# A recommender tower on one Trainium2 core: block writes on ScalarE's queue, first rows in runs of 24, 8 and 7 fields, gathers placed between lows, dense block loaded in turn 30

## The reference, cut to what matters

```python
e = jnp.stack([tbl_0[ids[:, 0]], ..., tbl_38[ids[:, 38]]], axis=1)          # (2048, 39, 16)
for idx, (W, b) in enumerate([(w0, b0), (w1, b1), (w2, b2)]):               # x0 = xk = e at first
    z = relu(jnp.einsum('bhd,bkd,hks->bsd', x0, xk, W) + b[None, :, None])   # s = 128
    if idx != 2: xk = z[:, :64, :]; direct.append(z[:, 64:, :])
    else: direct.append(z)
h = jnp.concatenate([jnp.sum(jnp.concatenate(direct, 1), axis=-1), dense_ctx], axis=1)   # 256 + 16
y = relu(relu(h @ W_top1 + b_top1) @ W_top2 + b_top2) @ W_top3
```

## Time and profile before

| what | us |
|---|---|
| median of 3 runs (2551.67 to 2557.73) | 2557.03 |
| the profiled execution: its own time | 2558.01 |
| the profiled execution: span from first to last instruction | 2556.2 |
| PE busy, of the span | 2407.8 (94%) |
| DVE busy | 2251.4 (88%) |
| POOL busy | 1689.2 (66%) |
| ACT busy | 1058.5 (41%) |
| first squared product on DVE starts at | 99.11 |
| layer 2 of turn 0, 1, 2, 3, 4, 5 read out by ACT at | 209.7, 292.4, 365.3, 442.0, 515.0, 587.4 |
| the same of turn 30 and 31 | 2413.6, 2496.4 |

### The profile page before, as it was taken

The page is one execution under the profiler, slowest core; times in us unless marked ns, Lnnn a source line. Parts: engine busy times, 40 slices in busy tenths (PEclk is TensorE's granted clock), DMA queues, the critical chain, the costliest instruction groups (busy, mean ns, idle before and its releaser), DMA issues.

```text
span 2556.2 us, 30130 instructions
## 1 busy us (share of the span) xinstructions
PE 2407.8 (94%) x7702; PEld 1448.5 (57%) x7702; DVE 2251.4 (88%) x1657; ACT 1058.5 (41%) x1053; POOL 1689.2 (66%) x1059
## 2 busy tenths in 40 slices
PE   0389999999999999999999999999999999999889
PEld 0145665555666565655666555556665565666556
DVE  0279998999999999999999999999999998999973
ACT  0133444444444444444444444444444443444345
POOL 7267676776767677776768777677768776444330
PEclk9999999999999999999999999999999999999989
DMA  7547998788899888888898888888988887898810
GB/s 185 123 97 183 215 200 192 184 192 198 194 214 202 196 198 194 200 192 199 199 215 194 196 201 191 201 193 199 216 200 201 190 199 162 198 211 198 185 42 11
DMA packets 177592, 470.31 MB, mean 184 GB/s; under 512 B 33972, under 2 KB 68148, under 8 KB 177230
## 3 DMA queue, kind: packets, MB, share of 16 engines
q1 hardware_dynamic: 155249, 462.10, 78.3%
q0 software_dynamic: 19968, 5.15, 2.0%
q10 hardware_dynamic: 2286, 2.23, 0.4%
HBM read 457.02 MB, written 12.33 MB: 184 GB/s over the span
## 4 chain that ended last, share of the span: by engine, by line
PE 67%; POOL 12%; issue 8%; DVE 3%; DMA 1%; ACT 0%; POOLq 0%; SPq 0%; ACTq 0%; DVEq 0%
PE zacc_a L1011 28%; PE zacc_b L1011 26%; POOL low L643 6%; POOL landed L621 5%; PE zacc_a L1046 5%; PE zacc_b L1046 5%; DMA x_thrice<-in_w_top1d 1%; DVE prod L911 1%; DVE low L866 1%; POOL mark L627 1%; PE zacc_b L1043 0%; PE zacc_a L1043 0%; DVE zacc_a L915 0%; DVE prod L915 0%; PE maps L1053 0%
## 5 line engine op out<-in xcount | busy, mean ns | idle before, releaser
L643 POOL TENSOR_TENSOR low<-prod,high 128x1024 fp32r<-128x1024 f32 x384 | 944.8, 2470 | 610.6 <-ACT high L798 604.1
L911 DVE TENSOR_TENSOR prod<-spread,maps 128x2048 f32<-128x2048 f32 x448 | 1016.8, 2281 | 94.1 <-issue 25.5
L798 ACT ACTIVATE high<-prod 128x1024 fp32r<-128x1024 f32 (+1 forms) x576 | 596.1, 1056 | 717.7 <-DVE prod L911 385.2
L1011 PE MATMUL zacc_a<-prod,w_plain 128*128 128x512 f32 (+2 forms) x1536 | 708.8, 596 | 47.1 <-DVE prod L896 41.2
L621 POOL DMA_INDIRECT landed<-in_tbl,rows_id x585 | 631.3, 1079 | 166.4 <-issue 150.8
L1011 PE MATMUL zacc_b<-prod,w_plain 128*128 128x512 f32 (+2 forms) x1536 | 709.0, 596 | 5.9 <-DVE prod L911 5.9
L1011 PEld LDWEIGHTS zacc_a<-prod,w_plain 128*128 128x128 f32 (+2 forms) x1536 | 291.9, 190 | 318.1 <-issue 290.7
L1011 PEld LDWEIGHTS zacc_b<-prod,w_plain 128*128 128x128 f32 (+2 forms) x1536 | 292.1, 190 | 276.4 <-issue 248.9
L896 DVE TENSOR_TENSOR prod<-shifted,x_thrice 117x1024 f32<-117x1024 f32 (+1 forms) x224 | 265.4, 1221 | 88.6 <-DMA shifted<-x_periods 72.9
L1046 PE MATMUL zacc_b<-low,w_high 128*128 128x512 f32 x672 | 283.0, 502 | 14.8 <-POOL low L643 8.6
L1046 PE MATMUL zacc_a<-low,w_high 128*128 128x512 f32 x672 | 280.6, 498 | 6.8 <-POOL low L643 6.8
(11 more groups left out here) (103 smaller groups left out, 1627.8 us busy)
## 6 DMA issues: line engine op xcount, KB each, us to landing
spread<-x_periods SPq DMA_DIRECT2D x608, 512.0 KB, 17.3
shifted<-x_periods SPq DMA_DIRECT2D x628, 156.0 KB
x_thrice<-x_periods SPq DMA_DIRECT2D x93, 156.0 KB
landed<-in_tbl,rows_id POOLq DMA_INDIRECT x585
spread<-x_periods SPq DMA_DIRECT2D x32, 256.0 KB
x_periods<-x SPq DMA_DIRECT2D x30, 256.0 KB, 3.9
spread<-features SPq DMA_DIRECT2D x4, 512.0 KB, 4.7
features<-feat ACTq DMA_DIRECT2D x15, 128.0 KB
```

Of the source, the lines that this page charges most:

```text
L643: nc.gpsimd.tensor_tensor(low[0:rows, at_, :], prod[0:rows, at_, :], high[0:rows, slot(j, SPLIT, NH), :], ALU.subtract).then_inc(s_lowp, 1)
L798: nc.scalar.activation(high[0:rows, h, :], made(turn, j)[0:rows, :], ACT.Copy).then_inc(s_round, 1)
L911: nc.vector.tensor_tensor(prod[:, at_:at_ + 2, :], spread[:, t:t + 2, :], maps[:, :].unsqueeze(1).to_broadcast([128, 2, COLS]), ALU.mult). ...
L1011: return nc.tensor.matmul(z[:, hf * BANK:(hf + 1) * BANK], w, x[:, hf * BANK:(hf + 1) * BANK], start=start, stop=stop)
```

## The change

Six edits, all outside the shared loop:

1. `write_block` is issued by ScalarE, right behind its copy of the block, and each block has a semaphore of its own; SP only waits for it.
2. `EARLY_BLOCKS` goes from 3 to 2: eight spread loads are issued in the start and not twelve; four more follow later, behind the squared tiles.
3. The rows of `x_thrice` and `shifted` come in three parts (fields 0 to 23 after block 2, 24 to 31 after block 3, 32 to 38 after block 4) and not in two. The run lengths change accordingly: 24; 21 + 3; 18 + 6; 15 + 9, then 8 everywhere, then 7 (and 1, 6, 2, 5). Of the last part ScalarE's queue takes u = 0 and 2, SP the rest.
4. 25 gathers of group 1 are issued ahead, the other 14 at the tiles of `SECOND_AT`; group 2's follow a table written out by hand. The turning, copying and writing of group 1 move by one tile (27, 28, 29).
5. `load_context` and GpSimd's clearing move from turn 31, j = 0, to turn 30, j = 27; ScalarE's five steps move from tiles 6, 8, 12, 14, 16 to 3, 6, 8, 12, 14.
6. GpSimd's last subtraction waits for VectorE's last low.

```diff
-TURN0_AT, COPY0_AT, WRITE0_AT, GATHER0_AT = 26, 27, 28, 27
-GATHERED_AHEAD = 20
-EARLY_BLOCKS = 3
+TURN0_AT, COPY0_AT, WRITE0_AT, GATHER0_AT = 27, 28, 29, 28
+GATHERED_AHEAD, SECOND_AT = 25, (1, 5, 9, 10, 10, 13, 14, 17, 19, 21, 21, 23, 25, 26)
+EARLY_BLOCKS = 2
...
-CTX_AT = (6, 8, 12, 14, 16)
+CTX_AT = (3, 6, 8, 12, 14)
...
+        PARTS = [(0, 3 * len(BLOCKS[0])), (3 * len(BLOCKS[0]), 4 * len(BLOCKS[0])), (4 * len(BLOCKS[0]), FIELDS)]
+        def runs_of(shift, part):
+            lo, hi = PARTS[part]
+            runs = [(max(0, lo + FIELDS * k - shift), min(FIELDS, hi + FIELDS * k - shift)) for k in range(PERIODS)]
+            return [run for run in runs if run[0] < run[1]]
...
             for q in range(TURNED):
-                write_block(q)
-                sp.wait_ge(s_first_w, 16 * PERIODS * (q + 1))
+                sp.wait_ge(s_first_w[q], 16 * PERIODS)
                 if q < EARLY_BLOCKS:
                     for piece in (2 * q, 2 * q + 1):
                         load_spread(Turn(None, 0), piece)
-                elif q < TURNED - 1:
-                    load_thrice0(sp, 0)
-                    for u in range(RING0):
-                        load_shifted0(sp, u, 0)
                 else:
-                    load_thrice0(sp, 1)
-                    load_shifted0(sp, 0, 1)
+                    load_thrice0(sp, q - EARLY_BLOCKS)
+                    for u in range(1, RING0, 2) if q == TURNED - 1 else range(RING0):
+                        load_shifted0(sp, u, q - EARLY_BLOCKS)
...
+                if turn.fixed and turn.number() == CHUNKS - 2 and j == LAST[0]:
+                    load_context()
                 if turn.fixed and turn.number() == CHUNKS - 1:
-                    if j == 0:
-                        load_context()
...
-                if turn.fixed and turn.number() == 0 and GATHERED_AHEAD + j < FIELDS:
-                    gather_second(GATHERED_AHEAD + j)
-                if turn.fixed and turn.number() == CHUNKS - 1 and j == 0:
+                if turn.fixed and turn.number() == 0 and j in SECOND_AT:
+                    for n in range(SECOND_AT.index(j), SECOND_AT.index(j) + SECOND_AT.count(j)):
+                        gather_second(GATHERED_AHEAD + n)
+                if turn.fixed and turn.number() == CHUNKS - 2 and j == LAST[0]:
                     pool.wait_ge(s_square, CHUNKS * N0)
...
+            pool.wait_ge(s_lowv, n_kind(Turn(None, CHUNKS - 1), LAST[-1], ON_DVE) + 1)
             pool.wait_ge(s_cast_top, 2)
             nc.gpsimd.tensor_tensor(m_w2l, m_w2, m_w2h, ALU.subtract).then_inc(s_top, 1)
...
             for q in range(TURNED):
                 copy_block(q)
+                if q < TURNED - 1:
+                    act.wait_ge(s_first_x, q + 1)
+                else:
+                    act.wait_ge(s_x, 1)
+                write_block(act, q)
...
-            act.wait_ge(s_first_w, 16 * PERIODS * TURNED)
-            for u in range(1, RING0):
-                load_shifted0(act, u, 1)
+            act.wait_ge(s_first_w[-1], 16 * PERIODS)
+            for u in range(0, RING0, 2):
+                load_shifted0(act, u, 2)
```

More of the change, by code:

```diff
@@ L149, in gather_slots @@
     return sorted(among + [rest[i * len(rest) // need] for i in range(need)])
-GATHERS, GATHERS0 = gather_slots(GATHER_AT), gather_slots(GATHER0_AT)
+GATHERS = gather_slots(GATHER_AT)
+GATHERS0 = (28, 28, 29, 31, 32, 33, 36, 37, 38, 39, 44, 47, 48, 52, 54, 58, 61, 61, 61, 66, 67, 68, 68, 69, 70, 74, 74, 75,
+            78, 80, 81, 85, 86, 89, 89, 91, 91, 91, 92)
 DOUBLED = pairs()
@@ L271, in build @@
         s_first_x = sem("s_first_x")
-        s_first_w = sem("s_first_w")
+        s_first_w = [sem(f"s_first_w{q}") for q in range(TURNED)]
         s_all = sem("s_all")
@@ L458, in chunk0, with load_thrice0, load_shifted0, write_block @@
             return flat[first:first + rows, 0:COLS]
-        def load_thrice0(engine, late):
+        def load_thrice0(engine, part):
             for s in range(PER0):
-                for lo, hi in thrice_rows(s, late):
+                for lo, hi in runs_of(FIELDS - s, part):
                     engine.dma_start(x_thrice[s * FIELDS + lo:s * FIELDS + hi, :], chunk0(FIELDS - s + lo, hi - lo)
                                      ).then_inc(s_thrice, 16)
-        def load_shifted0(engine, u, late):
+        def load_shifted0(engine, u, part):
             for s in range(PER0):
-                for lo, hi in square_rows(u, late):
+                for lo, hi in runs_of(PER0 * u, part):
                     engine.dma_start(shifted[s * FIELDS + lo:s * FIELDS + hi, u, :], chunk0(PER0 * u + lo, hi - lo)
                                      ).then_inc(s_shifted[u], 16)
+        def write_block(engine, q):
+            rows = min(128, FLAT - 128 * q)
+            for k in range(PERIODS):
+                engine.dma_start(x_periods[0, k, 128 * q:128 * q + rows, :], x[0:rows, q, :]).then_inc(s_first_w[q], 16)
         @block.sync
@@ L514, in load_first @@
             def load_first(n):
-                if n.fixed and n.number() < 2:
-                    sp.wait_ge(s_first_w, 16 * PERIODS * TURNED)
-                else:
+                if not n.fixed or n.number() > 1:
                     sp.wait_ge(s_written, n.group(32 * PERIODS, 0))
@@ L680, in emit @@
                         f = places.index(turn.odd * TILES + j)
-                        gather(f, f + 1)
+                        gather(f, f + places.count(turn.odd * TILES + j))
             turns(pool, emit, GROUPS - 2)
+            pool.wait_ge(s_lowv, n_kind(Turn(None, CHUNKS - 1), LAST[-1], ON_DVE) + 1)
             pool.wait_ge(s_cast_top, 2)
@@ L747, in copy_x @@
                 if n.fixed and n.number() < 4:
-                    act.wait_ge(s_first_w, 16 * PERIODS * TURNED)
+                    for q in range(TURNED):
+                        act.wait_ge(s_first_w[q], 16 * PERIODS)
                 else:
```

21 lines of the change are left out of this document (2 added, 19 removed).

## The result

The changed kernel takes 2520.2 us (median of 4 runs, 2519.77 to 2523.6) against 2554.4 for the kernel before, made beside it. The ratio is 0.9868, 95% interval [0.9851, 0.9886]. It is faster by 34 us where 59 were forecast, and 5 us above the end of my range. The profiled execution has a span of 2518.2 us, 38.0 less than before.

The account below looks back on a forecast made before the run. TensorE, fully busy in the loop, was taken as the bound, so only its idle times outside counted: 34 + 10.5 + 12.9 + 1.5 = 58.9 us off 2558.01 gives 2499.1, stated as 2498 us; range 2485 to 2515.

Parts of the forecast that it names:

- first square earlier: Start: the first squared product begins at about 65 us instead of 99.1, a gain of 34 us.
- turns 0 and 1: Waits on lows of tiles 11 and 17 and at turn 1's head go: 6 - 1 + 5.5 = 10.5 us.
- dense load: Turn 31: loading the dense weights in turn 30 removes TensorE's wait of 10.84 us, a gain of 12.9 us.
- last low: Before the MLP: GpSimd's last subtraction no longer precedes VectorE's last low, removing TensorE's 1.55 us wait; 1.5 us.
- Step (b): Start: SP issues 24 loads of fields 0 to 23 at 0.40 us each, 9.6 us, to 55 us.
- step (d): Start: SP issues 15 loads at 0.35 us, then 11 at 0.33, to 64; first square about 65 us.
- (a): Start: blocks 0 and 1 go as before, at most 3 us earlier; block 2's write lands at 45 us.
- (c): Start: block 4's gathers land sooner, so it is turned at 54.5 us and its write landed by 58.
- The reading behind it: Start before: 29- or 23-row loads are served by one DMA engine, SP blocked behind its backlog; 156 rows, 22 us.
- tiles 40 and 41: Turn's last tiles: four gathers instead of three ahead of these lows cost TensorE at most 1.25 us, taken as -1.
- The short loads queue too: Rival, start: short loads issue slowly too; at 0.66 us each 2511 (chance 0.14), at 1.31 us 2544 (chance 0.05).
- the lock of turn 1: Rivals: GpSimd's lows still delay VectorE's, 2505 (POOL or lock, 0.12); or 6.2 us in 28 loop turns, 2672 (0.03).

Follow-up runs that it names:

- e14: Changed kernel with GpSimd waiting for the first square only ahead of field 10 of group 1's gathers, at about 65 us; 2487.1 us.
- e15: Changed kernel with a 128x512 memset on GpSimd behind each of group 1's gathers from field 10 on; 2495.4 us.
- e9: Kernel before with the 29- and 23-row runs cut into 28 + 1 and 22 + 1, the same rows in 27 issues for 21; 2532.8 us.
- e3: Kernel before with the new gather places and group 1's turning, copying and writing at tiles 27, 28, 29 alone; 2539.5 us, ratio 0.9941.
- e4: Kernel before with the dense block loaded in turn 30 (and ScalarE's steps moved) alone; 2541.2 us, ratio 0.9948.
- e8: Kernel before with group 1's gathers held back until the first square; 2564.1 us.
- e12: Kernel before with the new gather places, the earlier dense load and the last subtraction's wait, the start unchanged; 2523.5 us, ratio 0.9877.
- e10: Changed kernel with a 128x512 memset on GpSimd behind each of group 1's 25 early gathers; 2498.1 us.
- e13: Changed kernel with group 1's gathers held back until the first square; 2500.6 us, ratio 0.9784.
- e2: Changed kernel with x_thrice and shifted loaded in 15 whole runs of 39 rows, all behind block 4; 2489.7 us, ratio 0.9748.
- e7: Changed kernel with ScalarE's queue taking u = 0 and 2 of all parts of the loads, not only the last; 2510.9 us.
- e18: The program of e14 run again in another set, on the same chip; 2504.1 us, ratio 0.9803.
- e17: Changed kernel unedited, run again in the last set; 2517.8 us, ratio 0.9838.
- e5: Changed kernel unedited, run again in the second set; 2519.6 us, ratio 0.9855.

## Why the prediction was wrong

| term | forecast | changed kernel | e14 and e15 |
|---|---|---|---|
| first square earlier | 34 | 3.8 | 33.5, 33.6 |
| turns 0 and 1 | 10.5 | 19.2 | |
| dense load | 12.9 | 12.6 | |
| last low | 1.5 | 1.6 | |
| MLP (no edit's doing) | 0 | 1.7 | |

**Step (b) failed**, the 24 loads at 0.40 us each. The first three took 0.38, the other 21 took 1.22 and lasted to 71.8, and the 15 of step (d) likewise to 92. Steps (a) and (c) came in at 45.07 for 45 and 52.9 for 54.5, and the last 11 loads at 0.30 for 0.33. Where the issuing was quick, e14 and e15 had their first square at 65.6 and 65.5, against 65, and took 2487.1 and 2495.4 against 2498. The step was thus a fair one for executions with quick issuing, which no trace of the unedited changed kernel shows. The totals say less than the first square: the 8.3 us between e14 and e15 are the uneven middle (2042.6 and 2051.0), and turns 0 and 1 gave more than forecast.

**The reading behind it was half right.** One engine's backlog was real (e9) and the new runs remove it. But the trace of before held a second cause, hidden under the first: its 21 loads took 27.56 us where the same loads took 18 to 19 in e3, e4, e8 and e12. It cost the kernel before nothing, and the changed one some 30 us of its start (first square at 95.3, and at 65.6 in e14). Its median of 0.700 us on SP was no mixture of quick and blocked loads. It was the grid of 0.7 us that the changed kernel shows, and half of the slow loads had only three to nine rows, as I wrote under the rivals and then explained away. Blocked loads look different: in e12 the median is 0.307 and the longest 3.906. (The row count behind the prediction's estimate of 27 us has a slip too: its 171 + 17 rows for the kernel before leave out 12 of `x_thrice` and of u = 0, which the 39 + 15 + 17 for the new one count. With them it is 200 rows and 29 us; nothing else hangs on it.)

**The list of waits was read too kindly.** "Between 219 and 2432 it holds only small ones" is wrong: one of 6.16 us stands at 2146.78. The change doesn't reach it, as the prediction says, so the sum is not touched.

**Turns 0 and 1: right places, a term left out.** The waits were 6.05 and 6.23 us, forecast 6 and 5.5; two small ones of 0.77 together went as well, and the cost of tiles 40 and 41 was 0.28 for 1. The other 3.8 and 2.4 us are the clock that TensorE lost behind the two long waits. I had seen it in the same rows (1.22 for a pair against 0.73) and counted it at the end of the program but not here.

**The end** came as forecast. The 1.7 us of the MLP are the clock of the one profiled execution of before, as e3 and e4 show.

**The rivals.** "The short loads queue too" was what happened, but not by its mechanism, and between its two prices: by 1.31 us a load it gave 2544, because it let all 50 loads go at that pace and left out the clock. Of the others none came: GpSimd's gathers ended at 86.7, 34 us before its first low, the lock of turn 1 went, and no turn of the loop had it. In versions with a quick start and late gathers GpSimd did become late: TensorE waits 3.60 us for a low in e10 and 10.24 in e13.

## What to carry to other kernels

Look at the median and the longest issue of a queue before naming its cause: a few issues of 4 us among many of 0.3 are a blocked engine, all of them at 0.7 and 1.4 are a slowed queue, and one cure doesn't help the other. Prefer few whole loads with a row count that shares out well (39, 28, 24) to many early pieces; here 15 whole loads behind the last block were even with 50 pieces begun 10 us earlier and issued quickly (layer 2 of turn 0 at 167.2 in e2, 167.4 in e14), with far fewer loads to be slowed. A wait of TensorE can cost more than its length: here those of 4.50, 6.23 and 10.84 us cost 3.8, 2.4 and 1.7 more in lost clock, and one of 1.55 cost 1.6 in one execution and nothing elsewhere. And an experiment that was quick once should be run again beside the unedited kernel, in one set, before a theory rests on it.

## What the runs showed of the hardware

- SP's and ScalarE's plain loads have two paces of issue: about 0.35 us, and a grid of 0.70 and 1.40 us (1.2 to 1.5 on the mean). The slow one was seen only with GpSimd's gathers running, begins after the first five loads or so of a queue (nine in e7 on ScalarE), ends 4 to 7 us after the gathers (4.2 in e18, 5.4 in the changed kernel, 6.4 in e17, 6.7 in e5), and does not come in every set of executions, for one program on one chip.
- A load of 29 or 23 rows of 4 KB runs on one engine at about 7 rows per us (13 packets from 75 to 77 us in e8, 6.5% of 16 engines). 156 such rows held a write behind them by 13.5 us; cut to 28 + 1 and 22 + 1, by 2.8.
- TensorE's granted clock was 0.50 from 159.16 to 163.00 us and from 218.57 to 222.00, right behind waits of 4.50 and 6.23 us, and 1.00 from 145.98 to 154.66, behind one of 1.55; in the MLP's first 10 us, behind another of 1.55, it was 0.82 (2496.39 to 2506.00), and 1.00 in e3 (2478.92 to 2488.50), behind one of 1.53. Over the stretches of 53 and 40 us this made 0.87 and 0.91.
